# ScalarE's one-hots put ahead of the next tile's mean, and the routed rows' list made ahead of the schedule, in a graph layer on one core

## What is computed

```python
xn = _layernorm(x)
h = xn @ W_self.T + (segment_sum(xn[src], dst) / deg) @ W_neigh.T + bias
x = x + layernorm(h) * gamma + beta + linear_attention(xn)   # 8 heads, elu + 1 features
t = _layernorm(x)
probs = softmax(t @ gate_w.T + gate_b); top_v, top_i = top_k(probs, 2)
x = x + shared_experts(t) + sum over k of top_v[k] * routed_expert[top_i[k]](t)
```

## Time and profile before

| | us |
|---|---|
| median of 3 runs | 2250.5 (2247.77 to 2253.26) |
| the profiled execution's own time | 2250.51 |
| its span, first to last instruction | 2248.9 |

### The profile page before, as it was taken

One profiled execution on the slowest core, in us unless ns is written; L12 is line 12 of the kernel. 1 busy time (PEld: TensorE's weight loads), 2 busy tenths in 40 slices (PEclk: granted clock), 3 DMA queues, 4 the chain that ended last, 5 costly groups with the idle time before them and its releaser, 6 DMA issues. The chain is left out here.

```text
span 2248.9 us, 46227 instructions
## 1 busy us (share of the span) xinstructions
PE 2042.3 (91%) x12932; PEld 1367.6 (61%) x12933; DVE 1551.8 (69%) x3789; ACT 1082.8 (48%) x2118; POOL 1275.6 (57%) x1370
## 2 busy tenths in 40 slices
PE   4898897899999999999999999983999999789998
PEld 2544454566666666666666666652666666557776
DVE  6888896577877788778877887874444444346666
ACT  3555664555646564656565556522343434223332
POOL 3665665777777777777777777711322222243433
PEclk9999999899999999999999999996999999899999
DMA  8637553788888888888888888852554545567775
GB/s 278 223 113 250 189 184 117 218 272 262 257 263 270 263 261 266 268 262 257 266 261 254 256 268 253 262 199 94 155 164 156 162 155 163 155 195 254 246 263 194
DMA packets 190000, 497.24 MB, mean 221 GB/s; under 512 B 42012, under 2 KB 54812, under 8 KB 188152
## 3 DMA queue, kind: packets, MB, share of 16 engines
q0 software_dynamic: 92720, 309.47, 46.4%
q1 hardware_dynamic: 66505, 135.52, 17.3%
q10 hardware_dynamic: 30719, 51.60, 6.1%
HBM read 373.91 MB, written 122.50 MB: 221 GB/s over the span
## 5 line engine op out<-in xcount | busy, mean ns | idle before, releaser
L665 POOL DMA_INDIRECT region<-table,idx x122 | 116.5, 955 | 356.2 <-PE bank L1312 268.8
L625 POOL DMA_INDIRECT region<-table,ebuf x225 | 225.5, 1002 | 82.6 <-issue 81.7
L625 POOL DMA_INDIRECT Wff<-table,ebuf x225 | 218.4, 971 | 74.0 <-issue 73.4
L334 PE MATMUL bank<-Wff,region 128*125 128x512 f16 (+1 forms) x636 | 245.1, 385 | 13.1 <-DVE region L2061 8.0
L335 PE MATMUL bank<-Wff,region 128*125 128x512 f16 (+1 forms) x636 | 244.1, 384 | 0.0
L336 PE MATMUL bank<-Wff,region 128*125 128x512 f16 (+1 forms) x636 | 244.0, 384 | 0.0
L632 POOL DMA_INDIRECT Wff<-table,ebuf x200 | 196.6, 983 | 61.0 <-issue 60.4
L632 POOL DMA_INDIRECT region<-table,ebuf x200 | 193.8, 969 | 61.0 <-issue 61.0
L1149 PE MATMUL bank<-region,ohs 128*125 128x512 f16 x850 | 192.4, 384 | 10.5 <-DMA region<-table,ebuf 10.4
L1149 PE MATMUL bank<-Wff 128*125 128x512 f16 x850 | 188.3, 380 | 0.0
L2026 DVE COPY region<-bank 128x1024 f16<-128x1024 f16 x60 | 41.5, 692 | 178.4 <-PE bank L1312 178.4
(11 more groups left out here) (327 smaller groups left out, 5504.5 us busy)
## 6 DMA issues: line engine op xcount, KB each, us to landing
yd<-region ACTq DMA_DIRECT2D x59, 512.0 KB, 3.1
x2d<-region SPq DMA_DIRECT2D x25, 512.0 KB
table<-region SPq DMA_DIRECT2D x25, 512.0 KB, 4.6
region<-x2d SPq DMA_DIRECT2D x25, 512.0 KB, 5.1
table<-region POOLq DMA_DIRECT2D x50, 250.0 KB, 3.4
xnt<-region POOLq DMA_DIRECT2D x25, 500.0 KB, 4.0
region<-xnt SPq DMA_DIRECT2D x25, 500.0 KB, 5.4
x2t<-region SPq DMA_DIRECT2D x25, 500.0 KB
```

What stands on the lines that cost most here:

```text
L334: wmm(ps, xh, wh, start=first, stop=False)
L625: pool.indirect_dma_start(out=ring[j][:, s, :], out_offset=None, in_=table, in_offset=bass.IndirectOffsetOnAxis(ap=ebuf[j][:, 2 * s:2 * s ...
L665: pool.indirect_dma_start(out=tg[:, c, :], out_offset=None, in_=table2, in_offset=bass.IndirectOffsetOnAxis(ap=idx[:, 2 * turn + c:2 * tur ...
```

## The change

It has two parts. In ScalarE's `group` the call `onehots(later, 0)` is put ahead of `means(nxt, 0)`. At the end of the second stage VectorE makes the list of indices right behind the rounds' first step, then the sum of the rounds and `sched2`, and the places of the nodes last. SyncE issues the first copy of indices before it looks at the schedule, and loads the last two blocks of weights only in front of expert 1, when three is reached by `rows_landed` (it starts at 2 and is raised once for every round whose rows have landed). GpSimd reads the schedule behind its first two gathers.

```diff
@@ SyncE
-            sp.wait_ge(sem["agg_end"], NT)
-            sp.wait_ge(sem["spread_ps"], 2 * NG)
-            sp.wait_ge(sem["slot_ps"], 2 * NG)
-            part = slice((OVER - 2) * FFB, OVER * FFB)
-            sp.dma_start(over[:, part], ffd[:, part]).then_inc(sem["ff_back"], 16)
+            sp.wait_ge(sem["idx_set"], 2)
+            sp.dma_start(idx[:, 0:2], idx_all[:, 0:2]).then_inc(sem["ix_in"], 16)
             sp.wait_ge(sem["agg_end"], NT)
             sp.wait_ge(sem["sched2_set"], 1)
-            sp.wait_ge(sem["idx_set"], 2)
             for e in range(NE):
+                if e == 1:
+                    sp.wait_ge(sem["spread_ps"], 2 * NG)
+                    sp.wait_ge(sem["slot_ps"], 2 * NG)
+                    sp.wait_ge(sem["rows_landed"], 3)
+                    part = slice((OVER - 2) * FFB, OVER * FFB)
+                    sp.dma_start(over[:, part], ffd[:, part]).then_inc(sem["ff_back"], 16)
                 lo = sp.value_load(...)
                 hi = sp.value_load(...)
-                if e == 0:
-                    sp.dma_start(idx[:, 0:2], idx_all[:, 0:2]).then_inc(sem["ix_in"], 16)
@@ GpSimd
-            pool.wait_ge(sem["sched2_set"], 1)
-            total = pool.value_load(sched2[0:1, NE:NE + 1], min_val=2 * NE, max_val=400)
             pool.wait_ge(sem["ix_in"], 16)
             pool.nop().then_inc(sem["ix_taken"], 1)
             rows_of(0, 0)
+            pool.wait_ge(sem["sched2_set"], 1)
+            total = pool.value_load(sched2[0:1, NE:NE + 1], min_val=2 * NE, max_val=400)
@@ ScalarE, group(i, prev, nxt, later)
+                if later is not None:
+                    onehots(later, 0)
                 if nxt is not None:
                     means(nxt, 0)
-                if later is not None:
-                    onehots(later, 0)
                 normalised(i)
@@ VectorE, the order of its steps behind L1986
-            places shifted (L1988, L1993 to L1999), rounds summed (L2005, L2006), pos_all, sched2, list out of bank 7 (L2013), indices (L2015)
+            list out of bank 7, indices, rounds summed, sched2, places shifted, pos_all
```

More of the change, by code:

```diff
@@ L1986, in _ @@
             ts(sched2[:, 0:NE], CN[:, 0:NE], -0.5 + 0.5 / CH, 2.0, ALU.add, ALU.max).then_inc(stepped, 1)
+            dve.wait_ge(sem["slot_ps"], 2 * NG)
+            listed_ids = gelc.rearrange("p c n -> p (c n)")[:, 0:COLS // 2].bitcast(F16)
+            dve.tensor_copy(listed_ids, bank[7][:, 0:COLS]).then_inc(sem["idx_set"], 1)
+            dve.wait_ge(sem["idx_set"], 1)
+            ts(idx_all, listed_ids.bitcast(I16), -float(ID_BASE), 0.0, ALU.add, ALU.max).then_inc(sem["idx_set"], 1)
+            dve.wait_ge(stepped, 4)
+            dve.tensor_copy(KA[:, 1:NE + 1], sched2[:, 0:NE]).then_inc(stepped, 1)
+            ts(SH[:, 0:NE], sched2[:, 0:NE], float(CH), -float(CAP), ALU.mult, ALU.add).then_inc(stepped, 1)
+            a, b, d, n = KA, KB, 1, 6
+            while d < NE + 1:
+                dve.wait_ge(stepped, n)
+                dve.tensor_copy(b[:, 0:d], a[:, 0:d]).then_inc(stepped, 1)
+                tt(b[:, d:NE + 1], a[:, d:NE + 1], a[:, 0:NE + 1 - d], ALU.add).then_inc(stepped, 1)
+                a, b, d, n = b, a, 2 * d, n + 2
+            dve.wait_ge(stepped, n)
+            dve.tensor_copy(sched2[:, 0:NE + 1], a[:, 0:NE + 1]).then_inc(sem["sched2_set"], 1)
             dve.wait_ge(sem["gate_dve"], GATE_STEPS * NG)
             dve.tensor_copy(P0, pos[:].rearrange("p t k -> p (t k)")).then_inc(stepped, 1)
-            dve.wait_ge(stepped, 5)
-            dve.tensor_copy(KA[:, 1:NE + 1], sched2[:, 0:NE]).then_inc(stepped, 1)
-            ts(SH[:, 0:NE], sched2[:, 0:NE], float(CH), -float(CAP), ALU.mult, ALU.add).then_inc(stepped, 1)
+            dve.wait_ge(stepped, n + 1)
             dve.tensor_copy(P2, P0).then_inc(stepped, 1)
-            n = 8
+            n += 2
             for e in range(1, NE):
@@ L2000, in _ @@
                 n += 2
[L2002 to L2007, removed]
             dve.wait_ge(stepped, n)
             dve.tensor_copy(pos[:].rearrange("p t k -> p (t k)"), P2).then_inc(sem["pos_set"], 1)
[L2010 to L2015, removed]
             dve.wait_ge(sem["agg_end"], NT)
```

## The result

The median of four runs is 2326.6 us (2323.5 to 2328.4) against 2250.7 for the kernel before, beside it on the same chip: a ratio of 1.0336, interval 1.0318 to 1.0354. The forecast was 2328. The profiled execution took 2325.5 us with a span of 2323.9. In the new file the lines around the change have moved: `turn_mean` is L1206, ScalarE's mean L828, the one-hots L818 and L820, the shift of `iota_f` L1717, the aggregation L1147, `turn_rows` L1310.

What follows compares the result with a forecast made beforehand. Three engines had groups of nearly one length, TensorE busiest, so any new TensorE wait over 1.5 us lengthens the second stage. 2250.5 + 46 (loop) + 36 (clock) - 4.5 (between stages) = 2328 us, range 2282 to 2360.

Steps and rivals of the forecast that it cites:

- The closed loop: Second stage, node-number shift through both `turn_mean`s and back to the shift: 46.6 us a group against 44.54.
- The term of +46 us: Second stage, groups 0 to 22: the longer loop costs 23 x 2.0 = 46 us, bounds 32 to 67.
- The wait: TensorE at the first `turn_mean`: new wait of about 3.7 us for ScalarE's mean; the second's 1.5 us wait goes.
- The clock: TensorE after its new idle time: falls to half clock in 17 of 23 groups, 2.1 us each, +36 us.
- Part two: Between second and third stage: first rows land 6.2 us earlier, weights' load costs 1.7; -4.5 us, between -6.2 and -1.8.
- The load beside the gathers: Between the stages: loading the last weights while round 1's gathers fly costs 1.7 us, bounds nothing to 4.4.
- the 8.46 us of the nearest row: A traced gather beside about 2 MB of loads, 8.46 us against 4.08: upper bound of 4.4 us more for the load.
- a gather slowed twofold: Skill's DMA page: queues alternate packets, so a gather wholly beside the weights' load costs 4 us more; between-stages change then -2.2.
- The clock that stays up: Rival: TensorE's clock does not fall, or falls seldom, after the new idle time; 2292 us, chance 0.22.
- A fall in every group: Rival: TensorE's clock falls in every group, with long half-clock stretches, 62 us; 2354 us, chance 0.1.
- The mean is still in time: Rival: first `turn_mean` does not wait and the second's 1.5 us goes, 35 us off; 2211 us, chance 0.05.

Runs made afterwards that it cites:

- the kernel with filler: Changed kernel with 44 extra unused matmuls before the first `turn_mean` of every group, shortening TensorE's idle time: 2286.2 us, ratio 1.0149.
- the order alone: Kernel before with only ScalarE's order changed, one-hots ahead of the next mean: 2335.2 us, ratio 1.0366.
- (-8.6 to -3.8) by the run: Changed kernel with ScalarE's order put back, so only the part between second and third stage is changed: 2245.6 us, ratio 0.9973.
- the run with the load in front: Kernel with early list and ScalarE's old order, with the last weights' load put back ahead of the first index copy: 2249.4 us, ratio 0.9996.
- the kernel with own node numbers: Changed kernel with a separate node-number table for each of a group's two tiles, each moved by 250 after its own count: 2240.2 us, ratio 0.9947.
- Splitting the add: The kernel with own node numbers, its VectorE add of beta and bias to x split: two pieces 2227.5 us, four pieces 2221.8 us.

## Why the prediction was right

- **What bounds the group.** The closed loop was the right thing to add up. In the kernel with filler, where the clock is out of it, the pieces are 8.06 us (shift to first `turn_mean`), 11.26 (to the second), 11.63 (to the end of `of_mean(1)`), and 15.36 (second row of h to the end of the shift), against 8.1, 11.4, 11.7 and 15.4. Each is a little smaller; the sum is 46.3 for 46.6. The term of +46 us measured 40.5.
- **The wait.** 0.30, 7.04 and 0.72 us against 0.3, 7.03 and 0.74; TensorE idle 3.2 us for 3.7, as it comes to `turn_mean` a little later than I had it.
- **The clock.** +36 forecast, 40.4 to 41.6 measured, but as 22 x 1.84 and not 17 x 2.1: more falls, each cheaper, as 17 of 22 were the short kind. The two errors partly cancel, which is luck. That every group falls is what the page "TensorE: Matmul & The Clock Gate" of the Trainium skill, section "Why this matters for your kernels", would have had; this trace agrees, with 22 of 22 at 3.2 us idle, and the order alone nearly so, with 20 of 22.
- **Part two.** -4.5 forecast; -5.9 at the first turn of rows and some +0.8 behind it (the second turn starts 9.29 us behind the first, 8.53 before) in the trace, -6.3 (-8.6 to -3.8) by the run. The load beside the gathers was priced at 1.7 us and cost 0.8: the gather on the path took 4.46 us beside it (1636.68 to 1641.14), and the one before it, without the load, 4.30. Neither the 8.46 us of the nearest row nor a gather slowed twofold showed. The step that failed here is the view of the load as a cost only: by the run with the load in front, it would have held up the early copy of indices for 6.45 us, and 4.5 of the 5.9 us hang on moving it.
- **The rivals.** The clock that stays up was priced at 2292 and is the kernel with filler: 2286. A fall in every group is what came (22 of 22), but with 5 long stretches, not 23, so not at its 2354. "The mean is still in time" at 2211 is the kernel with own node numbers: there the mechanism holds (no `turn_mean` waits), and the price fails, because the 1.5 us were divided between TensorE and a GpSimd that is bound at 44.2 us. I had estimated GpSimd's group at 43.8 us and then left it out of that rival.

The sum 46 + 36 - 4.5 = 77.5 measured 40.5 + 40.4 - 6.3 = 74.6, and 75.9 in one piece. The mechanisms of the loop and of the clock were right, but that the time came within 2 us of the forecast is luck: the loop was 5.5 us too high, the clock some 5 us too low. The low end of the range was also added up wrongly: it takes 38 us for the loop, where the working gives 32 (2276, not 2282).

Open: why the order alone skipped the fall in two groups with the same wait, and why five of the 22 stretches at half clock were longer. Nothing was run for either.

## What to carry to other kernels

Before work is moved into an engine's idle time, look at what ends that idle time and whether the moved work reads the same thing. Here the one-hots waited for a counter one instruction away from what the mean needed, and 7 us of work came between the mean and an engine with 3.9 us of slack. Then price a wait of TensorE by what the clock does behind it as well: half of this loss was the clock, and 2 us of idle work in front of the wait would have bought it back. Where several engines have groups of nearly one length, removing a wait gives only the distance to the next engine, so work that out for each of them first.

## What the runs showed of the hardware

A gather issued by GpSimd is held up by an operation on VectorE with two operands in SBUF that runs when it starts: 0.95 us become up to 1.94, and it ends 0.82 to 0.83 us behind the operation's end, for adds of 1.21 and 0.42 us alike. An add with one operand in PSUM leaves it at 0.95 to 0.96 (26 of 26). Two tensors from SBUF are not the whole condition: in the kernel before, all 10 gathers that start during a float16 TENSOR_SCALAR over 400 columns (L1865, `Wff<-Wff,posc`) take 1.04 to 1.05 us and end 0.82 to 0.83 us behind it too. Splitting the add was worth 11.2 us in two pieces and 19.4 in four. The page "SBUF — State Buffer" of the Trainium skill, section "Who interferes with whom", names the ports that the two engines share and says that the loser waits for the whole instruction; the rows agree. The same section says that two SBUF operands hold up a GpSimd instruction that reads SBUF, but infers that such an add leaves GpSimd's making of DMA descriptors alone; for these indirect gathers the rows differ from the inference, by 0.98 us.

A copy of 1 KB of indices took 6.45 us when it was issued 1.0 us behind the load of 2 MB on the same queue, and 1.2 to 1.8 us without one beside it. But the copy for round 2, issued 2.1 us behind the same load in the kernel after, took 2.39 us; why these two differ stays open. And TensorE's clock fell to half behind each of 22 idle times of 3.2 us in the changed kernel and behind 20 of 22 in the order alone; behind 1.2 us, with the filler, in 21 of 22 groups it didn't.
